# Last graph layer: the first projection's rows are copied whole to SBUF, and its dot products are taken head by head from the copy

## The reference

```python
h = (x @ W).reshape(n, heads, out_c)            # 625 x 8 x 96
al_s = jnp.einsum('nhc,hc->nh', h, a_src)
al_d = jnp.einsum('nhc,hc->nh', h, a_dst)
e = jax.nn.leaky_relu(al_s[src] + al_d[dst], NEG_SLOPE)
m = jax.ops.segment_max(e, dst, num_segments=n)
ex = jnp.exp(e - m[dst])
z = jax.ops.segment_sum(ex, dst, num_segments=n)
alpha = ex / (z[dst] + 1e-16)
msg = h[src] * alpha[:, :, None]
out = jax.ops.segment_sum(msg, dst, num_segments=n)
```

## Time and profile before

| | us |
|---|---|
| median of 3 runs | 1730.11 (1727.32 to 1731.02) |
| the profiled execution's own time | 1730.77 |
| its span in the trace | 1728.9 |
| DVE busy in the span | 846.0 (49%) |
| PE busy in the span | 1524.1 (88%) |

### The profile page before, as it was taken

How to read it: one execution, slowest core, us unless ns; L and a number is a source line. 1 busy time by engine, 2 the same in 40 slices (tenths; PEclk the granted TensorE clock), 3 DMA queues, 4 the chain that set the end, 5 groups by cost and what they waited for, 6 DMA issues and landing times.

```text
span 1728.9 us, 26969 instructions
## 1 busy us (share of the span) xinstructions
PE 1524.1 (88%) x10142; PEld 1475.4 (85%) x10142; DVE 846.0 (49%) x2128; ACT 587.6 (34%) x1172; POOL 528.5 (31%) x681
## 2 busy tenths in 40 slices
PE   3988999998879999887999999999999998676787
PEld 3767889997879989887999999999999997666687
DVE  5887776325467753354532313141322215599743
ACT  3335444323344543222323232222232122366521
POOL 3235234232233332232213233323234231222222
PEclk9979999999889999997999999999999999768898
DMA  2222111123211111232112122112132222100012
GB/s 88 84 75 62 37 44 46 54 75 95 70 49 49 44 43 50 68 111 83 36 29 65 44 66 65 51 52 63 40 99 84 73 79 77 52 1 1 1 56 91
DMA packets 88125, 101.64 MB, mean 59 GB/s; under 512 B 9593, under 2 KB 80744, under 8 KB 87997
## 3 DMA queue, kind: packets, MB, share of 16 engines
q1 hardware_dynamic: 71986, 71.20, 14.3%
q10 hardware_dynamic: 16011, 28.73, 5.2%
HBM read 88.12 MB, written 11.78 MB: 58 GB/s over the span
## 4 chain that ended last, share of the span: by engine, by line
PE 59%; DVE 15%; issue 10%; ACT 6%; DMA 5%; POOL 4%; DVEq 1%; ACTq 0%; POOLq 0%; SPq 0%
PE ps L850 36%; PE ps L1049 7%; PE ps L1031 4%; PE ps L935 4%; DVE prob L1951 3%; DVE junk L1900 3%; DMA xl<-x_scratch 2%; PE ps L902 2%; DVE prob L1959 2%; PE ps L1070 2%; PE ps L1093 1%; DMA xl<-in_x 1%; POOL pairs L1172 1%; PE ps L873 1%; ACT pairs L1261 1%
## 5 line engine op out<-in xcount | busy, mean ns | idle before, releaser
L1172 POOL TENSOR_TENSOR pairs<-stage,pairs 128x256 fp32r<-128x256 f32 (+3 forms) x472 | 372.7, 807 | 791.8 <-ACT pairs L1261 790.7
L850 PE MATMUL ps<-pairs,XB 128*125 128x256 f32 (+2 forms) x2760 | 402.0, 306 | 26.4 <-issue 15.0
L850 PEld LDWEIGHTS ps<-pairs,XB 128*125 128x125 f32 (+1 forms) x2760 | 390.8, 193 | 30.0 <-issue 16.7
L850 PE MATMUL ps<-pairs,XA 128*125 128x256 f32 (+4 forms) x2595 | 367.4, 302 | 6.4 <-DVE XA L1584 2.3
L850 PEld LDWEIGHTS ps<-pairs,XA 128*125 128x125 f32 (+2 forms) x2595 | 361.3, 187 | 8.4 <-issue 2.8
L1261 ACT ACTIVATE pairs<-stage 128x256 fp32r<-128x256 f32 (+3 forms) x472 | 188.1, 423 | 510.7 <-PE ps L850 388.5
L1584 DVE TENSOR_TENSOR Hl<-ps,Hl 125x768 fp32r<-125x768 f32 (+3 forms) x57 | 43.6, 818 | 269.7 <-ACT Hl L1313 269.7
L935 PE MATMUL ps<-AT,Hg 125*128 125x314 f32 (+1 forms) x1080 | 168.4, 316 | 3.8 <-DVE rl L1987 3.8
L935 PEld LDWEIGHTS ps<-AT,Hg 125*128 125x128 f32 (+1 forms) x1080 | 163.3, 192 | 4.8 <-DVE rl L1987 3.7
L1219 POOL TENSOR_SCALAR prob<-prob,rden 125x625 f32<-125x625 f32 x80 | 70.7, 884 | 228.6 <-DVE rden L1967 228.6
L902 PE MATMUL ps<-ident,prob 125*125 125x125 f32 x475 | 85.3, 327 | 47.9 <-POOL prob L1219 18.7
(11 more groups left out here) (219 smaller groups left out, 1661.2 us busy)
## 6 DMA issues: line engine op xcount, KB each, us to landing
stage<-in_W SPq DMA_DIRECT2D x192, 128.0 KB, 2.3
stage<-in_rel SPq DMA_DIRECT2D x99, 192.0 KB, 2.4
stage<-in_root SPq DMA_DIRECT2D x91, 64.0 KB, 1.8
x_scratch<-xo ACTq DMA_DIRECT2D x15, 375.0 KB
xl<-x_scratch ACTq DMA_DIRECT2D x15, 375.0 KB
stage<-in_rel SPq DMA_DIRECT2D x42, 128.0 KB, 2.1
stage<-in_root SPq DMA_DIRECT2D x12, 192.0 KB, 2.4
stage<-in_W SPq DMA_DIRECT2D x12, 192.0 KB, 2.4
```

The lines of the kernel that those rows point to most:

```text
L850: last = mm(o, X[:rows, xi, a, P * (s0 + t):P * (s0 + t) + m], pair(n, b), start=k == 0 and i == 0 and t * pitch % BANK == 0, stop=k == le ...
L1172: nc.gpsimd.tensor_tensor(pair(n, 1), staged(n), pair(n, 0).bitcast(F32), ALU.subtract).then_inc(*up("weights_lo", "weights lo", n))
```

## The change

Five things change, all in block 3's first layer, and no matmul is added or removed.

- ACT writes the rows of both halves twice: whole, as fp32, to a new buffer `full3` in SBUF, and then the high halves as before. The PSUM banks are free after the high halves' copy. `full3` lies where `XA` tiles 2 to 5 will be, so the elu outputs of heads 2 and 4 wait for its readers.
- `rows_lo` and the dots read `full3` and not PSUM.
- The dots are cut by head (`head_dots`, 10 instructions each). Heads 0 and 1 come ahead of the loop, head 0 even ahead of `rows_lo`, heads 2 and 3 in ticks 1 and 2, heads 4 to 7 in ticks 15, 20, 25 and 30.
- TensorE does one weight tile of the second half ahead of head 0's `spread`, where it did two.
- `rows` of a projection no longer asks for splits; three `split` steps and, for the second layer's first five weight tiles, one `split_to` in each of the ticks 8, 11, 14, 17 and 20 do. The second half's `rows` moves from tick 2 to 3, its `rows_lo` to tick 6.

```diff
     if l == 3:
-        yield ("project", l, 0, 384)
-        yield from rows_of(("project", l, 0, 384))
-
-        yield ("part", ("project", l, 1, 384), 0, 2)
-        yield from (("score_sum", l, 0), ("spread", l, 0), ("scores", l, 0), ("mask_rows", l, 0, 0))
-        yield ("project", l, 1, 384)
-        yield ("split", ("project", l, 1, 384), 1)
+        first, second = ("project", l, 0, 384), ("project", l, 1, 384)
+        yield from (("split", first, 4), first, ("rows", first), ("head_dots", first, 0), ("split", first, 6))
+        yield from (("part", second, 0, 1), ("score_sum", l, 0), ("rows_lo", first), ("spread", l, 0), ("scores", l, 0))
+        yield from (("head_dots", first, 1), ("mask_rows", l, 0, 0), second, ("split", second, 1))
 
         for t in range(heads * NT + 3):
             h, d = t // NT, t % NT
+            if t in (1, 2):
+                yield ("head_dots", first, t + 1)
+            if d == 0 and 3 <= h < heads - 1:
+                yield ("head_dots", second, h - 3)
+            if t >= 8 and t % 3 == 2 and t < 23:
+                yield ("split_to", ("project2", l, 0, 256), (t - 5) // 3)
...
-            if t == 2:
-                yield from rows_of(("project", l, 1, 384))
+            if t == 3:
+                yield ("rows", second)
+            if t == 6:
+                yield ("rows_lo", second)
...
-            elif s[0] == "rows" and s[1][0] == "project" and s[1][1] < 3:
+            elif s[0] == "rows" and s[1][0] == "project":
                 return 0
...
+        full3 = [sb(f"full3_{c}", [P, NT, 384], F32, o1 + (2 + 2 * c) * tile_b) for c in range(2)]
...
+                    if last_layer(s):
+                        A(full3[s[2]][:, s0:s0 + ns, :], psum_rows(q, ns, pitch, w), ACT.Copy).then_inc(
+                            *up("hi_ready", "rows full", s, g))
                     A(row_dest(s, s0, ns, 0, w), psum_rows(q, ns, pitch, w, rows_in(s, s0)), ACT.Copy).then_inc(
                         *up("hi_ready", "rows hi", s, g))
+                    if last_layer(s):
+                        G.same(("rows hi", s, g), "free", q)
...
+                    if l == 3 and h in (2, 4):
+                        act.wait_ge(*at("dots", ("project", 3, h // 2 - 1, 384)))
+                        act.wait_ge(*at("rows lo", ("project", 3, h // 2 - 1, 384), 2))
...
+                        if last_layer(s):
+                            rows = full3[s[2]][:, s0:s0 + ns, :]
...
+                elif kind == "head_dots":
+                    s, part = s[1:]
+                    i = gat_projects.index(s)
+                    if part == 0:
+                        dve.wait_ge(*at("vectors in", i, 1))
+                    for g, (s0, ns, pitch) in enumerate(groups(384)):
+                        if part == 0:
+                            dve.wait_ge(*at("rows full", s, g))
+                        for t in range(s0, s0 + ns):
+                            for v in range(2):
...
+                                V.tensor_tensor_reduce(
+                                    out=junk[:, j % 2, :96], in0=full3[s[2]][:, t, 96 * part:96 * part + 96],
+                                    in1=ab[:, i % 2, v, 96 * part:96 * part + 96], scale=1.0, scalar=0.0, op0=ALU.mult,
+                                    op1=ALU.add, accum_out=asp[:, v, 4 * s[2] + part, t:t + 1]).then_inc(
+                                    *up("rows_used", "dot", j))
...
-                    dve.wait_ge(*at("dots", last_piece(s)))
+                    if l == 3 and h < heads:
+                        dve.wait_ge(*at("head dots", l, h))
+                    else:
+                        dve.wait_ge(*at("dots", last_piece(s)))
```

More of the change, by code:

```diff
@@ L724, in copied, with last_layer @@
             return s[0] == "project" and s[-1] == 256
+        def last_layer(s):
+            return s[:2] == ("project", 3)
         def psum_rows(q, n, pitch, w, rows=P):
@@ L1879, in _ @@
                             G.same(("rows lo", s, g), "free", q)
+                elif kind == "head_dots":
[8 more added lines that the diff above has]
+                            for v in range(2):
+                                j = junks[0]
+                                junks[0] += 1
+                                if j >= 2:
+                                    dve.wait_ge(*at("dot", j - 2))
+                                V.tensor_tensor_reduce(
[3 more added lines that the diff above has]
+                                    *up("rows_used", "dot", j))
+                    G.same(("dot", junks[0] - 1), "head dots", 3, 4 * s[2] + part)
+                    if part == 3:
+                        G.same(("dot", junks[0] - 1), "vectors read", i)
+                        G.same(("dot", junks[0] - 1), "dots", s)
                 elif kind == "dots":
```

## The result

The changed kernel takes 1724.67 us (median of 22 runs, 1716.14 to 1728.53), the kernel before in the same comparison 1727.91 (median of 22, 1721.45 to 1734.3). The ratio is 0.9968, with an interval of 0.9957 to 0.9979: 0.32% faster, or 5.5 us (3.6 to 7.4). It compares the two sets of runs as wholes and isn't the quotient of the two medians: these are only 3.2 us apart, the means 4.9. The forecast was 6.0 us and 1724.1.

What follows compares the result with a forecast made beforehand. A chain with one engine working at a time bounds the start, DVE the loop behind it. Gains of 8.8 and 9.4 (18.2) less 12.2 given back make 6.0: 1730.77 to 1724.8 profiled, median 1724.1, range 1720.0 to 1728.6.

Steps and rivals of the forecast that it cites:

- The first mask: Start of block 3's first layer: DVE's first mask at 1486.8 instead of 1495.6, 8.8 us earlier.
- the collisions: Three POOL splits beside `rows_lo` and head 1's dots, both reading SBUF, cost DVE 0.69 each, 2.1 us in all.
- the upper bound: Upper end for a start collision: DVE loses the POOL operation's whole length, 1.3 us each.
- From the mask to the remainder: First mask to first transposed remainder on DVE: 14.3 us instead of 23.7, 9.4 more gained.
- The new wait for ACT: Ahead of the first transposed remainder DVE waits about 2.8 us for ACT's exp and second-half copies.
- Given back in the loop: DVE-bound loop: second `rows_lo` 2.2, 40 dots 7.1, POOL beside `rows_lo` 0.5, five splits 2.4; 12.2 us lost.
- The sum: Whole kernel: 18.2 gained less 12.2 lost, 6.0 us faster; chance 0.50.
- Collisions missed: Rival: POOL's splits miss DVE's SBUF reads at start and in loop; 1719.1 without any, 1721.6 with half; chance 0.20.
- Double cost: Rival: eight POOL splits cost DVE their whole length, or ACT's splits delay its queue; 1727.6; chance 0.14.
- Handed back whole: Rival: DVE's 5.42 wait ahead of the first mask returns behind the second half's copies; 1730.1; chance 0.06.
- Half-rate dots: Rival: dots read SBUF at half rate, adding 0.10 to each of 80, 8.2 us; 1732.3; chance 0.04.
- Lost phase: Rival: loop's DVE scores and masks shift beside POOL's scaling, up to 0.69 a tick; slower, 1747; chance 0.06.

Runs made afterwards that it cites:

- e13: Changed kernel with ACT's two high halves and POOL's three remainders at the start put behind head 0's `asb`; block start to second layer 161.67 us, changed kernel 159.10 at full clock.
- e6: Changed kernel without the rule that puts five of POOL's splits inside the loop; they run after the heads; ratio 0.9994.
- e4: Changed kernel with each of POOL's five splits inside the loop done twice; first block's start to second layer 162.54 us.
- e1: Kernel before with only the copy to `full3` added, its list of steps, splits and whole-row dots kept; ratio 1.0005.
- e2: Changed kernel with all 40 dots of the first half ahead of head 0's scores again; ratio 1.0007.
- e3: Changed kernel with dots of heads 2 and 3 moved to tick 3, where DVE waits 2.1; first transposed remainder at 30.44, against 30.16 at full clock.
- e11: Changed kernel with first-half and second-half dots moved into DVE's waits, ACT's vector load put off, five loop splits one a head in the elu wait's tick; ratio 0.9920.

## Why the prediction was right

**The first mask.** Forecast 8.8 earlier, measured 25.74 - 17.30 = 8.44. The chain it described (copy, ten dots, transposes, `asb`, `rows_lo`, ten dots) is the chain of the profile. Up to `rows_lo` it is right to 0.01: forecast 1480.7 - 1469.85 = 10.85 behind the block's start, measured 1476.20 - 1465.36 = 10.84. The slow clock early in the block did no harm, for the times of before that the forecast was built on had it as well, and from 1471 on the clock was 1.00, as assumed. The 0.36 that is missing lies between `rows_lo` and the mask, 6.46 instead of 6.1, and that is the collisions: put at 2.1, measured 2.45 (2.4 in e13), or 0.82 for each split of 1.0 and not 0.69, a bit nearer the upper bound.

**From the mask to the remainder.** Forecast 14.3, measured 14.40 against 23.74 before: 9.34 gained where 9.4 was said. The new wait for ACT was put at 2.8 and is 2.10, mainly because DVE lost 0.5 each in two meetings with POOL's scaling, for which the sum had nothing. The mask of 1.39 stands behind the exp that ACT's copies follow, and the wait absorbed it. The dot of 0.76 stands ahead of it and put the exp off: it began 9.31 behind the mask, where 9.0 was forecast. ACT's way from there was 0.2 shorter than forecast (5.09 instead of 5.3), so the total comes out by two small errors that cancel.

**Given back in the loop.** Forecast 12.2, measured 114.50 - 102.81 = 11.69, where 102.81 is before's 152.29 - 49.48. The dots cost 17.33 - 15.53 = 1.80 a head, where the forecast had 10 x 0.178 = 1.78. The second `rows_lo` took 2.79, where 2.2 + 0.5 stood. The splits cost 2.12 (e6) instead of 2.4, or 0.42 each. This term was the right kind and 0.3 too large. These parts make 7.2 + 2.8 + 2.1 = 12.1, so 0.4 of the forecast's excess of 0.5 is none of them. It lies ahead of the first once-a-head wait, where before has small waits that the sum left out: 0.30 for ACT at its second transposed tile, and a tick that is 0.2 longer than the same one in e6.

**The sum.** 8.44 + 9.34 - 11.69 = 6.09, and 0.11 from the tail: 6.20, against the forecast of 6.0. The comparison of all runs gives 5.5, with 3.6 to 7.4. The small errors (0.36 and 0.06 too high in the gain, 0.5 too high in the loss) cancelled in part, which is luck. So is some of the nearness of 1724.1 to the measured 1724.67: the forecast started from 1730.11, the median of three runs of before, and the 22 runs have 1727.91. From there the same 6.0 gives 1721.9.

**The rivals.** Collisions missed: they were not, e6 and e13 show 2.1 and 2.4. Double cost: no at the five small splits, which cost 0.42 each in e6 and where e4's second ones cost 0.30. (That rival's 2.5 should be 2.7, as 3.1 less 0.42.) Handed back whole: not here, but it is what happens in e1, which has the copy without the order. In e2 two thirds are handed back by the order, and the rest goes in the slow tail. Half-rate dots: no, 0.25 each with a step of 0.18 from SBUF, as from PSUM. The Trainium skill, "Vector Engine (DVE) Microarchitecture Reference", section "Points that are easy to get wrong", states the halving for one form of instruction, `S2S2D2_STT`; no run here shows whether the dots are of that form, so the trace speaks of the dots alone. Lost phase: head 7 takes 15.22, where it took 15.21 before.

**What it missed.** The sum had the loop's splits as a cost only. They are needed: without them 4.68 is lost ahead of the second layer. As the trace of before has these splits inside the loop as well, the difference between the kernels was not touched by it.

Not tried: the new order without the copy. By the kernel's text it can't run as it stands: TensorE's first piece of the second half, ahead of head 0's transposes, would need banks that the first half keeps until head 3's dots, and these stand in DVE's queue behind masks that need the transposes. An order that takes that piece later, with no copy, might have some of the gain; no run tells how much, so it is not shown that the gain needs the copy.

## What to carry to other kernels

When one engine bounds a loop, work moved into it costs its full length, unless it is issued right ahead of the instruction that waits: 40 dots cost 7.2 us at the head of a tick and 2.1 in front of the wait of 1.30. Before moving work into a wait, look at what the other engine has in its queue ahead of the instruction that ends the wait. In e3 that was a DMA issue which needed the moved work, and the wait merely moved. Freeing a resource earlier (the copy) gave nothing by itself; with the order that uses it the start moved.

## What was not expected of the hardware

A short DVE instruction with both operands in SBUF that meets POOL's subtraction of two SBUF operands can be longer by most of that subtraction's length: a dot of 0.25 took 1.05 to 1.07 beside a split of 1.0, three times in a row, and the splits kept their 2.99 for three. With longer DVE instructions both lose: `rows_lo` 3.92 instead of 2.29 and the splits 4.73 instead of 3.0. Beside masks and scores in e11 a split of 0.74 took 2.46 in five cases out of five and DVE lost nothing. A repeated split of 0.73 that fell into DVE's wait cost nothing (e4). So the price of a meeting is not a constant, and POOL's length alone doesn't tell it: DVE's has to be read beside it. I take it to depend on which engine is ahead and how densely DVE's instructions follow one another; no run here varied that by itself.

The first half's last block began at 1465.36 in the changed kernel and, in the eight trials that have its order there, anywhere from 1466.90 to 1476.55, although nothing ahead of it differs. That is more than the change's own effect: a difference of spans is not the effect of a change.
